# Attention inside a macaron block: the weighted values in three PSUM banks instead of one, and another order of additions and maxima on VectorE

## What is computed

```python
x = x + 0.5 * ffn(layernorm(x), w_gate, w_up, w_down)     # x: 4 x 2048 x 256
x = x + attn(layernorm(x), Wq, Wk, Wv)
x = x + 0.5 * ffn(layernorm(x), w_gate, w_up, w_down)

def attn(x, Wq, Wk, Wv):
    Q, K, V = x @ Wq, x @ Wk, x @ Wv
    scores = where(causal, Q @ K.T / sqrt(256), -inf)
    return softmax(scores) @ V

def ffn(x, w_gate, w_up, w_down):                          # F = 704
    # fp4_linear quantizes and dequantizes both operands in blocks of 16
    h = silu(fp4_linear(x, w_gate)) * fp4_linear(x, w_up)
    return fp4_linear(h, w_down)
```

## Time and profile before

| | us |
|---|---|
| runs shown | 1237.0, 1239.09, 1239.17 (median 1239.09) |
| the profiled execution, its own time | 1238.35 |
| its span | 1236.2 |
| mean granted TensorE clock, share of full | 0.992 |
| busy in the span: PE / DVE / ACT / POOL | 1163.4 / 1004.6 / 789.4 / 554.7 |
| attention, first scores to last weighted values | about 416 to 889 |
| FFN2, first down product to the end | 895 to 1236 |

### The profile page before, as it was taken

The page is one execution under the profiler, slowest core; times in us unless marked ns, Lnnn a source line. Parts: engine busy times, 40 slices in busy tenths (PEclk is TensorE's granted clock), DMA queues, the critical chain, the costliest instruction groups (busy, mean ns, idle before and its releaser), DMA issues.

```text
span 1236.2 us, 24519 instructions
## 1 busy us (share of the span) xinstructions
PE 1163.4 (94%) x7765; PEld 758.5 (61%) x7765; DVE 1004.6 (81%) x2809; ACT 789.4 (64%) x1599; POOL 554.7 (45%) x531
## 2 busy tenths in 40 slices
PE   1799999999998799999999999989899999999997
PEld 1366666666665566766676667656566666666664
DVE  6899999999998666466656655564789999999996
ACT  4768888888864355435444544564668888887863
POOL 2444554445444245434543543444344445455441
PEclk9899999999999999999999999999999999999999
DMA  6955544544444456546564656457245555555565
GB/s 214 248 102 85 95 88 91 95 94 84 89 85 91 84 117 112 111 101 109 106 125 99 112 95 127 88 97 120 45 83 112 121 121 110 112 114 108 121 123 113
DMA packets 462741, 134.35 MB, mean 109 GB/s; under 512 B 441297, under 2 KB 461905, under 8 KB 462673
## 3 DMA queue, kind: packets, MB, share of 16 engines
q1 hardware_dynamic: 454928, 125.62, 52.4%
q10 hardware_dynamic: 7744, 7.86, 2.0%
HBM read 11.34 MB, written 8.39 MB: 16 GB/s over the span
## 4 chain that ended last, share of the span: by engine, by line
PE 74%; DVE 13%; ACT 5%; issue 4%; SPq 2%; DMA 1%; POOL 1%; ACTq 0%; DVEq 0%; POOLq 0%
PE ps L1487 32%; PE ps L1448 17%; PE ps L1534 12%; PE ps L1522 9%; DVE arena L1138 2%; PE ps L1507 2%; PE ps L1500 2%; ACT arena L797 2%; DVE arena L1125 1%; DVE arena L1101 1%; ACT arena L789 1%; DVE arena L969 1%; DMA arena<-arena 1%; DVE arena L973 1%; SPq L418 1%
## 5 line engine op out<-in xcount | busy, mean ns | idle before, releaser
L1487 PE MATMUL ps<-wguT,arena 128*128 128x512 f16 (+1 forms) x2304 | 480.0, 363 | 5.2 <-DMA arena<-arena 4.4
L1487 PEld LDWEIGHTS ps<-wguT,arena 128*128 128x128 f16 x2304 | 226.1, 98 | 226.2 <-issue 7.2
L549 POOL TENSOR_TENSOR arena<-arena 128x704 f32<-128x704 f32 x128 | 193.4, 1511 | 253.6 <-DVE arena L982 253.6
L1448 PE MATMUL ps<-wdT,arena 128*128 128x256 f16 x2176 | 261.6, 275 | 15.2 <-DMA arena<-arena 6.6
L1448 PEld LDWEIGHTS ps<-wdT,arena 128*128 128x128 f16 x2176 | 213.5, 98 | 56.5 <-DVE x_sb L1040 10.0
L576 POOL TENSOR_TENSOR arena<-arena 128x128 f16<-128x128 f32 (+7 forms) x64 | 143.9, 2248 | 229.5 <-ACT arena L797 125.5
L806 ACT ACTIVATE arena<-ps,arena,cst 128x128 f16<-128x128 f32 (+7 forms) x64 | 80.5, 1258 | 192.1 <-DVE arena L1143 188.1
L1534 PE MATMUL ps<-arena 128*128 128x256 f16 x1632 | 188.8, 273 | 9.0 <-DVE x_sb L1154 9.0
L1522 PE MATMUL ps<-arena 128*128 128x512 f16 (+3 forms) x960 | 187.4, 347 | 3.5 <-ACT arena L797 3.5
L1534 PEld LDWEIGHTS ps<-arena 128*128 128x128 f16 x1632 | 158.2, 98 | 36.3 <-DVE x_sb L1154 12.4
L727 ACT ACTIVATE arena<-arena 128x704 int16<-128x704 f32 x128 | 100.8, 787 | 112.7 <-POOL arena L549 112.6
(11 more groups left out here) (132 smaller groups left out, 1423.1 us busy)
## 6 DMA issues: line engine op xcount, KB each, us to landing
out_dram<-x_sb SPq DMA_DIRECT2D x32, 256.0 KB, 2.7
x_sb<-in_L_attn_x_dram ACTq DMA_DIRECT2D x3, 2048.0 KB, 9.0
arena<-arena SPq DMA_TRANSPOSE x384, 3.5
arena<-arena SPq DMA_DIRECT2D x8, 256.0 KB, 2.9
arena<-arena SPq DMA_DIRECT2D x4, 512.0 KB, 3.1
x_sb<-in_L_attn_x_dram ACTq DMA_DIRECT2D x1, 1536.0 KB, 7.3
arena<-in_L_ffn_w_down_dram SPq DMA_DIRECT2D x1, 704.0 KB, 8.1
arena<-in_L_ffn_w_gate_dram SPq DMA_DIRECT2D x1, 640.0 KB, 4.4
```

Of the source, the lines that this page charges most:

```text
L549: g.tensor_tensor(hy[u].rearrange("p (j b) -> p b j", j=BL), h[u].rearrange("p (b j) -> p b j", j=BL), hri[u].unsqueeze(2).to_broadcast([P ...
L1448: i = nc.tensor.matmul(ps_dn[w % 2], hT[w][:, c * P:(c + 1) * P], wdT[:, k, :], start=(s == 0), stop=(s == len(DOWN_STEPS) - 1))
L1487: i = nc.tensor.matmul(psf[:, 1536 * u + lo:1536 * u + hi], xv[:, u, xl, kt, :], wguT[:, wl, lo // P:hi // P, kt, :], start=(s == 0), stop ...
```

## The change

Three edits go together.

1. `ps_o` becomes a list of three banks: 6, 2 and 7. `out_bank` picks bank 2 for tiles 0 and 2 of each batch, bank 7 for the last tile of the last batch, and bank 6 for all others. `weighted_values` waits for the addition of the last earlier tile in the same bank (`added_before`) instead of that of the tile before; the last tile has no such wait, but one for all `aux_lo`.
2. In `pe_pair` the first down product of FFN2 waits for one addition fewer (`NT` instead of `NT + 1`); the second now waits for `NT + 1`.
3. In `dve_slot`, slots 1, 4, 5, 6, 7 and 8 of each batch run softmax ahead of `aux_lo`; in slots 3 to 8 the addition comes ahead of `dve_z_stats` and `dve_z`.

```diff
-        ps_o = ps[:, 6, 0:D]
+        ps_o = [ps[:, k, 0:D] for k in (6, 2, 7)]
...
+        SCORES_FIRST = (1, 4, 5, 6, 7, 8)
...
+        def scores_first(s):
+
+            return s % TB in SCORES_FIRST
...
+        def out_bank(b, i):
+
+            if b == B - 1 and i % TB == TB - 1:
+                return 2
+            return 1 if i % TB in (0, 2) else 0
+
+        def added_before(b, i):
+
+            q = b * TB + i - 1
+            while q >= 0 and out_bank(q // TB, q % TB) != out_bank(b, i):
+                q -= 1
+            return q
...
-            V.scalar_tensor_tensor(xs, ps_o, ofac, xs, ALU.mult, ALU.add).then_inc(o_add, 1)
+            V.scalar_tensor_tensor(xs, ps_o[out_bank(b, i)], ofac, xs, ALU.mult, ALU.add).then_inc(o_add, 1)
...
-                    dve_attention_add(b * TB + t, t, (b * TB + t) * D)
-
-            if aux_first(s):
+                    dve_attention_add(b, t, (b * TB + t) * D)
+
+            if aux_first(s) and not scores_first(s):
                 aux_lo_part()
             if has_scores(s, last):
                 dve_softmax(q, s, b * NCHUNK + chunks_before(s))
             if not aux_first(s):
                 add_part()
+            if not aux_first(s) or scores_first(s):
                 aux_lo_part()
+            if aux_first(s) and s <= 2 * GT:
+                add_part()
             if has_z(s + 1, last) and s % GT == GT - 1:
                 dve_z_stats(g + 3, (g + 3) * (GT * D))
...
-            if aux_first(s):
+            if aux_first(s) and s > 2 * GT:
                 add_part()
...
                         nc.tensor.wait_ge(m_floor, 1)
                     else:
-                        nc.tensor.wait_ge(o_add, NT + 1)
+                        nc.tensor.wait_ge(o_add, NT)
                 if k == 5 and gp < NP:
                     nc.tensor.wait_ge(m_lo, 1)
+                if k == 5 and gp >= NP:
+                    nc.tensor.wait_ge(o_add, NT + 1)
...
             def weighted_values():
                 if t >= 0:
-                    nc.tensor.wait_ge(o_add, b * TB + (t + 1))
+                    if added_before(b, t) >= 0:
+                        nc.tensor.wait_ge(o_add, added_before(b, t) + 2)
+                    if out_bank(b, t) == 2:
+                        nc.tensor.wait_ge(aux_lo, B * NG * GT)
```

More of the change, by code:

```diff
@@ L1042, in dve_last_add @@
         def dve_last_add(i):
-            dve_attention_add((B - 1) * TB + i, i, ((B - 1) * TB + i) * D)
+            dve_attention_add(B - 1, i, ((B - 1) * TB + i) * D)
         def dve_pair(gp, qd, p, odd, start=None, x2=True, x3=True, end=False, adds=False):
@@ L1143, in dve_softmax, with dve_attention_add @@
             V.tensor_scalar(sbias[i % 2], smax, cst[:, C_M:C_M + 1], P_LN, ALU.mult, ALU.add).then_inc(s_bias, 1)
-        def dve_attention_add(q, i, col):
+        def dve_attention_add(b, i, col):
+            q = b * TB + i
             V.wait_ge(p_exp, q + 1)
@@ L1533, in pe_pv @@
                 vt = key_slot(k // GT, i) * GT + k % GT
-                m = nc.tensor.matmul(ps_o, pT[color(i)][pl][:, k, :], vs[:, vt, vl, :], start=(s == 0),
+                m = nc.tensor.matmul(ps_o[out_bank(b, i)], pT[color(i)][pl][:, k, :], vs[:, vt, vl, :], start=(s == 0),
                                      stop=(s == len(steps) - 1))
```

## The result

The changed kernel takes 1227.57 us (median of four runs, 1226.04 to 1229.3) against 1238.05 for the kernel before (four runs, 1236.03 to 1239.17): a ratio of 0.9917, 95% interval 0.9905 to 0.9929. It is faster, by 10.5 us. The forecast was a gain of 16.6, and 1222.2 us; the result lies 5.4 above it, just past the top of the range (1227.5). The profiled execution took 1227.53, its span is 1225.4, where before they were 1238.35 and 1236.2. So 10.8 us of the 16.6 of the sum are there, and 5.8 are not.

A forecast was written before the change was run, and what follows sets the result against it. PE, busy 94% of the span, was taken to bound the kernel, so its standstills could be won: -4.7 - 5.3 - 6.6 = -16.6 us, forecast 1222.2 us, range 1218.8 to 1227.5.

The forecast's parts named there:

- the sentence on the z transposes: Slot 4: dve_z 0.5 to 0.9 us later behind the addition, cover 0.4; cost nothing, at most 0.5 a batch.
- The forecast's own first sign of being wrong: PE waits on L418's transposes (z) in slot 8; listed first among the signs that the forecast is wrong.
- Slower: the z transposes late: Rival, 0.04: late z makes PE stand ahead of aux products of slots 8 and 12; 3.5 us lateness gives 1241.
- Batches 1 to 3: Waits ahead of tiles 1, 2 and 5 go, less 0.5 us for slot 9: -4.7 us in all.
- Slot 9: Its aux product waits for aux_lo of slot 8, now behind softmax: 0 to 0.2 us a batch, taken as 0.15.
- Last batch: Tiles 1 and 2 give 1.74 us; with the aux_lo and exp waits shortened, -5.3 in all (bounds 1.7 and 6.3).
- The chain: Last batch: exp, ACT preparations, high aux, aux_lo, maxima, next exp; softmax ahead of aux_lo cuts it in slots 4 to 8.
- Transition: Into FFN2: last tile's wait, the down product's pause and its half clock go, -6.6 us (bounds 4.8 and 6.9).
- VectorE's 99.6% in FFN2: Rival, 0.05: VectorE, 99.6% busy in FFN2, can't follow and the transition gives nothing: 1228.8 us.

The follow-up runs named there:

- z_first: The changed kernel with dve_z ahead of the attention addition again in slots 4 and 8; 1222.74 us, ratio 0.9881 to the kernel before.
- z_early: z_first with dve_z also ahead of aux_lo in the first slot of the first batch; 1222.22 us, ratio 0.9864 to the kernel before.
- z_early_slot4: z_slot4 with dve_z also ahead of aux_lo in the first slot of the first batch; 1220.70 us, ratio 0.9877 to the kernel before.
- last_tile_only: Kernel before, with only the last tile's bank 7 without addition wait and the second down product taking the last addition's wait; 1232.44 us, ratio 0.9959.
- one_bank: z_first with bank 6 again for all tiles but the last, each waiting for the addition before; 1227.54 us, ratio 0.9915 to the kernel before.
- z_slot4: The changed kernel with dve_z ahead of the addition in slot 4 alone; 1222.30 us, ratio 0.9885 to the kernel before.
- banks_only: The changed kernel with VectorE's old order in all slots, keeping the three banks and the moved down-product wait; 1232.36 us, ratio 0.9954.
- adds_only: z_first with aux_lo ahead of softmax again in all slots but 0 and 2; 1230.42 us, ratio 0.9930 to the kernel before.

## Why the prediction was right or wrong

**The step that failed** is the sentence on the z transposes: "POOL's low part of z waits at this time for POOL's own work on tile 4; I cost it at nothing, and at up to 0.5 a batch at the far end." I took POOL's work on tile 4 as cover for a later `dve_z`. It was no cover: it was what `dve_z` ran into. Against z_first, and counted from the first scores, `dve_z` of the second batch starts 0.88 later (551.57 - 416.85 against 550.01 - 416.17), as the order asks, and grows by 1.09; ACT and POOL come behind it, and the transposes leave 1.74 later (557.34 and 554.92). Cost: 3.2 us in three waits, and 0.9 for slot 9 of the last batch behind them.

That the later place alone would have cost next to nothing, as forecast, is an estimate from rows of the changed kernel and of z_first: `dve_z` of 1.37 from 551.57 on, then 0.04 to ACT, 1.06 for ACT's part, 0.08 to POOL and 2.13 for POOL's part give transposes 0.6 later than in z_first (counted from tile 13 of the batch before). In z_first the last z transpose lands 0.85 ahead of need in the second and last batch and 0.41 in the third. So 0.4 us in all for the place, and some 2.8 of the 3.2 for the collision. I had counted that POOL would be busy, and not that it would be busy at the same time as `dve_z`. The forecast's own first sign of being wrong, PE waiting on the z transposes in slot 8, is what came. Two rows of the kernel before, second batch, would have shown how near they were:

```profile
549.85 1.37 DVE L1117 TENSOR_SCALAR arena<-x_sb,arena 128x256 f32<-128x256 f32 x4
```

```profile
551.85 1.40 POOL L576 TENSOR_TENSOR arena<-arena 128x640 f16<-128x640 f32 x1 [2.25 <-ACT arena L806]
```

They pass each other by 0.63 us, and the addition put ahead of `dve_z` takes, with its two small steps, 0.84 (550.73 to 551.57). And the same trace had shown such a collision elsewhere. L1022, another `tensor_scalar` of VectorE from SBUF to SBUF, has a median of 0.33 us, but once took 1.63, beside POOL:

```profile
402.83 1.58 POOL L549 TENSOR_TENSOR arena<-arena 128x704 f32<-128x704 f32 x1 [1.30 <-DVE arena L982]
```

```profile
402.97 1.63 DVE L1022 TENSOR_SCALAR arena<-arena 128x704 int16<-128x704 int16 x1
```

The view of the line tells of it: 325, 332 and 1631 ns, shortest, median and longest.

The Trainium skill has this rule (SBUF — State Buffer, section "Who interferes with whom"): a `tensor_scalar` of VectorE in a mode that uses both its ports to SBUF shares one of the two pairs with GpSimd, as an exclusive lock; whichever comes first holds it for its whole instruction, and the other blocks. The traces agree: 2.46 against 1.37, and 1.37 again when either order or a wait keeps them apart; and in two places an instruction of `dve_z` that had begun first held up POOL's (last section). That `dve_z` runs in such a mode is inferred, and no row shows it.

**The rival "Slower: the z transposes late"** named the place and the direction, PE standing ahead of the aux product of slot 8, but not the cause. Its rule (a lateness, less the cover, and the restart) holds with measured numbers: against z_first the last transpose lands 1.71, 1.90 and 1.71 later, z_first has 0.85, 0.41 and 0.83 of it to spare, and the rest is the 0.86, 1.50 and 0.88 lost. I had put 4% on it, as a case that must outweigh all; as a partial loss it should have stood in the range. Its other sentence, that above 3 us a pause brings the half clock, was read from one row, and the runs don't bear it out as a rule (last section).

**Batches 1 to 3.** The waits ahead of tiles 1, 2 and 5 are gone and the four ahead of tile 13 stand (0.32, 0.33, 0.33, 0.65), as said. Slot 9 costs 0.21, where I took 0.15. In batch 1 0.92 won ahead of the scores of tile 3 (which I hadn't counted) is lost again ahead of slot 4, for the z transposes there (4.43 in place of 3.45). The size of the gain was right once z was mended (2.05 for 2.1), its reason was half wrong: I gave it to the banks, and it needs the cut ring too.

**Last batch.** The chain is cut as described: the 1.85 is gone and the 0.86 stays. `act_p_hi` of tile 7 starts at 788.54, between the 787.7 and 788.6 forecast, but that is luck, for the forecast's clock had not been set forward for the start of attention nor back for the batches ahead. Counted from tile 13 of the third batch it comes 1.5 earlier than before, where I said 2.0 to 2.9 (z_first: 3.2), and that of tile 8 comes 4.5 earlier, where I said 4.9 to 5.8 (z_first: 5.9). 4.54 of 5.3, and 5.87 in z_first: the term was right within its bounds, and what it lacks against z_first is z.

**Transition.** PE's timeline after, to be laid beside the earlier trace rows:

```profile
876.25 5.40 PE L1559 MATMUL ps<-arena 128*128 128x256 f16 x48
881.49 3.73 PE L1512 MATMUL ps<-wguT,arena 128*128 128x512 f16 x18
885.38 2.02 PE L1471 MATMUL ps<-wdT,arena 128*128 128x256 f16 x17 [0.17 <-DMA arena<-arena]
887.23 3.73 PE L1512 MATMUL ps<-wguT,arena 128*128 128x512 f16 x18
```

6.52 for 6.6: no wait ahead of the last tile, a wait of 0.17 for the transpose of h, and the full clock. VectorE's 99.6% in FFN2 took nothing back: from 887.23 to the last gate product all stays 11.6 to 11.7 earlier.

**Outside attention.** The start gave 1.13 away, and the last down products 0.9. I had allowed for neither at the top of the range, though the runs of before alone spread by 3. z_first lacks the second, has 0.45 of the first, and lies at 1222.74, 0.5 above the forecast.

## What to carry to other kernels

When an instruction is moved, ask not only who waits for it, but what runs on the other engine in its new place: here VectorE's `tensor_scalar` of 0.41 us from SBUF to SBUF stood until GpSimd's `tensor_tensor` was over. Compare the longest instruction of a line with its median; a few that are several times longer can tell of such a collision. Where an instruction comes near one, as `dve_z` in slot 8 of z_first does (it ends at 570.98, POOL's work on tile 8 begins at 570.80), a shift of a microsecond elsewhere can bring it about. A wait that ends last in one slot may belong to a ring through several engines; freeing PE at one point is worth nothing until the ring is cut (here nothing and 5.4 us apart, 9.7 together). A change in two parts should be priced part by part in both orders.

## What the runs showed of the hardware

*VectorE and GpSimd.* The length of `dve_z` was 1.37 to 1.38 wherever POOL was idle, 2.45 beside a POOL instruction of 1.41, and 3.43 beside one of 2.37. POOL's own instruction mostly kept its length (1.41 and 1.40), but not where an instruction of `dve_z` that had begun first ran on beside it: in z_early, where this was 0.32 us, its low part of tile 0 took 0.60 where it is 0.43 elsewhere (that `dve_z` took 1.49), and in slot 8 of the changed kernel's third batch, with 0.28, that of tile 8 took 2.50 for 2.37. In slot 4, with 0.17, nothing was added. VectorE's instructions that read PSUM didn't grow: `aux_lo` took 0.68 at 562.95, while POOL's low part of tile 6 ran from 561.34 to 563.22. Nor is every pair from SBUF to SBUF affected: L1022 kept its 0.33 (at 912.41 in the kernel before) beside a POOL instruction of 0.69 that works on two elements a partition (L518), and the statistics (L1119) kept 0.41 the three times that POOL ran beside them in the changed kernel.

*The clock at the end.* The last two down products of the changed kernel, and a window on them (its length, busy time of PE, PEld, DVE, ACT and POOL, granted clock, DMA share, GB/s):

```profile
1216.73 5.54 PE L1471 MATMUL ps<-wdT,arena 128*128 128x256 f16 x34 [2.22 <-DMA arena<-arena]
```

```profile
1219.00:1222.00 3.00, 3.00 (x21) 2.27 (x19) 0.48 (x1) 0.00 (x0) 0.00 (x0) 0.67 0.08 26
```

In z_first the same two took 2.02 each at the full clock, behind nearly the same pauses (2.58 and 2.21). Of the thirteen profiles seven have the last two down products wholly or in part at half clock (1.2 GHz), which made the stretch from the start of the fourth last down product to the end of the last 0.8 to 1.0 us longer (14.3 to 14.4 for 13.4 to 13.5); the changed kernel has it both times. Two more have it one product earlier, where a wait behind it hides it. The Trainium skill (TensorE: Matmul & The Clock Gate, Part 1) says that where this falls varies from run to run; the rows show it between kernels of equal work, but what decides it here I can't show. The slow stretch at slot 4 of the first batch behaves likewise: its aux product took 2.57 to 2.72 behind pauses of 3.45 to 4.43, but 1.46 behind 3.98 in z_early_slot4 and 3.48 in last_tile_only. It also ends differently: the scores behind it take 1.79 at the full clock, and took 2.03 before, 2.18 in z_first, 3.24 in one_bank and 3.36 in z_slot4. Shorter pauses can bring it too: in last_tile_only the weighted values of tile 9 of the last batch, behind 1.85, took 5.12 where the kernel before has 3.45 behind the same pause, and in banks_only an aux product behind 2.11 took 2.47, in adds_only 1.47 behind 2.10. So no length of a pause tells the two apart in these rows.
